# Transposes of two 512 by 128 inputs moved from the matrix engine to memory and VectorE, in a graph network with a mixture of experts

## The chip, the cores and the metric

The kernel runs on one core of one Trainium2 chip. The metric is the device time of one execution in microseconds (us). A core has four compute engines that run their own instruction streams: TensorE (PE in the profile, with its weight loads as PEld), VectorE (DVE), ScalarE (ACT) and GpSimd (POOL). SyncE (SP) issues the DMAs, which 16 DMA engines carry out. Engines wait for each other by semaphores only.

## The reference

`x` is 16 batches of 512 nodes with 128 features, `adj` is 512 by 512. All is float32.

```python
def _layernorm(x, axis=-1, eps=1e-05):
    m = jnp.mean(x, axis=axis, keepdims=True)
    v = jnp.var(x, axis=axis, keepdims=True)
    return (x - m) / jnp.sqrt(v + eps)

# graph network, input x0 = layernorm(x)
h = jnp.einsum('bnd,ed->bne', x, fc_in_w) + fc_in_b
w_eff = w * d_clamped @ w.T
def euler_step(h, _):                       # 8 steps
    ax = jnp.einsum('nm,bmd->bnd', adj_mx, h)
    f = alph * 0.5 * (ax - h) + h @ w_eff - h + x0
    return (h + dt * f, None)

# experts, tokens z = layernorm(x + graph network)
logits = tokens.astype(jnp.float32) @ router_w.astype(jnp.float32).T
probs = jax.nn.softmax(logits, axis=-1)
rw, re = jax.lax.top_k(probs, TOP_K)        # 2 of 8 experts
...
for e in range(E):
    h = jax.nn.gelu(tokens @ w1[e] + b1[e], approximate=False)
    y = h @ w2[e] + b2[e]
    out = out + combine[:, e:e + 1] * y
...
x = x + gnn(layernorm(x)); x = x + ffn(layernorm(x))
```

## The kernel before, in words

**Groups.** The 16 batches are worked in 8 groups of GB = 2. A short set-up builds the operators: the 8 linear steps are folded into powers of the node operator (`LT`) and of the feature operator (`M`). Each float32 factor is split in a high part and a low part, and each product is three TensorE matmuls (`mm3`, L985 to L987). ScalarE makes the high part (`high`, L376), VectorE subtracts it for the low part (`low`, L550).

**One iteration.** Iteration g runs, on TensorE in this order: `nodes_product(3)` (12 matmuls, L985 to L987 with x0s); eight Q items of 9 matmuls (128x384), which read the transposed normalised input `GT[:, b, 0]` and three node products of it; two passes of `horner` (128x256); and then `experts(g-1)`, the experts of the group before. So the two halves of the network are one group apart: while the experts of group g-1 run, VectorE normalises the tokens z of group g and the kernel prepares group g+1. The iterations 1 to 6 are one loop body ("steady" in what follows; `more` is true in them); 0 and 7 are written out apart, and the experts of group 7 follow.

**Experts.** There are 16 items (2 batches by 8 experts). For item i TensorE makes the up product (3 matmuls on zT, w1s), ScalarE the gelu (L484) and the high part, VectorE the weighting `scale_item` (L854, which multiplies by the expert's weight of each token, broadcast to all partitions by DMA) and the low part `item_low` (L550, scs), and TensorE the down product (3 matmuls on scs, w2s), LAG = 5 items behind the up product. A down product waits for the low part of its item.

**Transposes.** The matmuls need the features on the partitions. `transpose_x0` (L1004) turns x0 of group g+1 and `transpose_z` (L1119) turns z of group g with TensorE, four 128x128 transposes for each batch, into PSUM banks; ScalarE and VectorE read them from there as high and low part. In a steady iteration z is turned after up products 10 and 11 and x0 after item 15. `transpose_out` (L1125) turns the experts' sums back.

**Routing.** `logits` (L1111, 8 matmuls) is issued after the first `transpose_out`. VectorE then runs `route_start` (one transpose of 128x256 and three small operations) and `route_on` in the parts 0 to 3 (5, 4, 4 and 4 small operations), each waiting for the one before: `route_start` after `add_out(h, 0)`, part 0 after the low parts of x0, part 1 between the low parts of the node products, and the parts 2 and 3 behind Q items 0 and 1 of the next iteration. The last one gives `comb_out`, which SP stores to memory (L298) and loads back broadcast to all partitions (L290).

**What sets the order.** The streams are written out by hand; each engine runs its instructions in that order and stands still at a wait. On SP, too, everything behind a wait waits.

Of the kernel before, what the change touches and what calls it, by code (L numbers as in the profile page):

```python
# [44 lines left out]
def build(nc, x, adj, alpha, w, d, fc_w, fc_b, router_w, w1, b1, w2, b2, comb_rows, out):  # L45
# [15 lines left out]
    with ctx:  # L61
# [31 lines left out]
        x0s = sb("x0s", [P, 2, NT, GB, D], F32R)  # L93
        GT = sb("GT", [P, GB, BABY, 2, N], F32R)
# [15 lines left out]
        shift = sb("shift", [P, T])  # L110
        zT = sb("zT", [P, 2, GB, N], F32R)
# [3 lines left out]
        lgT = sb("lgT", [P, T, R])  # L115
        cc = sb("cc", [P, T, 4, E])
        combT = sb("combT", [P, H], F32R)
# [59 lines left out]
        x0t_mm, x0t_hi, x0t_lo = sem("x0t_mm"), sem("x0t_hi"), sem("x0t_lo")  # L177
        gt_mm, gt_hi, gt_lo = sem("gt_mm"), sem("gt_hi"), sem("gt_lo")
# [8 lines left out]
        zt_moved = sem("zt_moved")  # L187
        lg_mm, rt_own, rt_pre, rt_tanh, comb_ready = (sem(n) for n in ("lg_mm", "rt_own", "rt_pre", "rt_tanh", "comb_ready"))
# [29 lines left out]
        Z_SCALE, Z_ITEM = 4, 10  # L218
        UP_BANK, SUM_BANK = [4, 5, 6], [0, 1]
# [32 lines left out]
        def _(sp):  # L252
# [39 lines left out]
            def expert_weights(h, g=None):  # L292

                sp.wait_ge(comb_ready, h + 1)
                for b in range(GB):
                    for half in range(2):
                        last = quarter(b, half) + R
                        sp.dma_start(comb_rows[bass.ds(h, 1), b, :, half * H:(half + 1) * H].rearrange("o e n -> (o e) n"),  # L298
                                     comb_out[last - E:last, :]).then_inc(comb_stored, 16)
                if g is not None:  # L300
                    sp.wait_ge(q_ready, T * g + T)
                else:
                    sp.wait_ge(sc_ready, ITEMS * h)
                sp.wait_ge(comb_stored, 64 * h + 64)
                if g is not None:
                    replicate(h, 0, 2, 0, 0)
                    replicate(h, 1, 4, 0, 2)
# [12 lines left out]
            with sp.Fori(1, GROUPS - 2) as g:  # L320
                expert_weights(g - 1, g)
                next_x(g + 2)
                store(g - 1)
            for g in range(GROUPS - 2, GROUPS):
                expert_weights(g - 1, g)
# [48 lines left out]
        def _(act):  # L374
# [29 lines left out]

            def high_gt(g, k, turn):
# [47 lines left out]
            def high_z(g, b, banks=ZT_BANK):  # L453
                act.wait_ge(zt_mm, GB * g + b + 1)
                high(zt_part(0, b), bank[banks[b]][:, :]).then_inc(zt_hi, 1)

# [20 lines left out]
            def experts(h, g=None, more=False):  # L477

                for i in range(ITEMS):
# [10 lines left out]
                    if i == Z_ITEM + 1 and g is not None:  # L490
                        high_z(g, 0)
                    if i == ITEMS - 4:
                        copy_sum(h, 0)
                    if i == Z_ITEM + 2 and g is not None:
                        high_z(g, 1)
                item_high(h, ITEMS - 1)
                if more:
                    high_x0t(g + 1)
# [766 lines left out]
```

## Time and profile before

| | us |
|---|---|
| median of 3 runs | 552.48 |
| lowest, highest | 551.25, 553.32 |
| the profiled execution, device time | 553.18 |
| its span from first to last instruction | 551.4 |
| TensorE busy | 536.2 (97%) |
| VectorE busy | 440.0 (80%) |
| ScalarE busy | 302.8 (55%) |
| GpSimd busy | 53.2 (10%) |
| DMA: share of 16 engines | 23.7% |
| mean granted TensorE clock | 0.996 |

The time is the profiled execution's own device time; the span is what the trace covers. The chain of work that ended last is 86% TensorE and 7% VectorE. In the timeline views a row gives its start and its duration; the next instruction of the same engine may start before the last one has ended, so the step from start to start is what an instruction takes from its engine, and start plus duration is when its result is there for others. An instruction of TensorE shows its latency; 128x512 matmuls follow each other every 0.23 us.

### The profile page before, as it was taken

The page shows a single profiled execution, that of the slowest core. Times are in us where ns is not written, and L with a number is a line of the kernel's source. Part 1 is how long each engine was busy: PE and PEld are TensorE (multiplying, and loading weights), DVE is VectorE, ACT ScalarE, POOL GpSimd, SP SyncE. Part 2 cuts the span into 40 slices and gives each one's busy share as a digit, 9 for nine tenths or more (in the row PEclk, how much of TensorE's full clock was granted, in tenths as well). Part 3 has the DMA queues.
Part 4 walks back from the last instruction along what each step waited for, and adds up shares of the span by engine and source line. Part 5 has one row for each costly group of instructions (what it writes and reads, how often), then busy time and mean ns, then how long its engine had stood idle before and what let it go on. Part 6 is the DMA issues. An engine that isn't in the chain of part 4 may idle for free.

```text
span 551.4 us, 9181 instructions
## 1 busy us (share of the span) xinstructions
PE 536.2 (97%) x2943; PEld 467.1 (85%) x2943; DVE 440.0 (80%) x1128; ACT 302.8 (55%) x525; POOL 53.2 (10%) x42
## 2 busy tenths in 40 slices
PE   5999999999999999999999999999999999999796
PEld 4788997988899788987899788987899788988585
DVE  6988778689866996689866996689866995489995
ACT  5323433468535783468535783468445782148584
POOL 1102011100110101110110101110110101010100
PEclk9999999999999999999999999999999999999999
DMA  4030010072104501172104501162104401160141
GB/s 128 4 112 1 0 40 0 23 246 79 39 3 152 190 0 38 30 244 71 38 2 152 190 0 38 38 236 71 38 2 152 152 4 35 59 233 17 42 191 39
DMA packets 26078, 43.15 MB, mean 78 GB/s; under 512 B 1622, under 2 KB 20684, under 8 KB 24140
## 3 DMA queue, kind: packets, MB, share of 16 engines
q1 hardware_dynamic: 26060, 42.93, 23.7%
q8 instruction: 9, 0.15, 0.1%
q14 instruction: 9, 0.07, 0.0%
HBM read 38.46 MB, written 4.46 MB: 78 GB/s over the span
## 4 chain that ended last, share of the span: by engine, by line
PE 86%; DVE 7%; issue 4%; ACT 2%; POOL 1%; DMA 1%; SPq 0%; POOLq 0%; DVEq 0%
PE bank L985 27%; PE bank L987 26%; PE bank L986 26%; DVE scs L550 2%; PE bank L1111 1%; DVE work L854 1%; PE bank L1125 1%; PE bank L1004 1%; PE bank L1119 1%; DMA work<-in_adj_dram 1%; DVE scr L579 1%; PE bank L1013 1%; PE bank L1171 1%; ACT x L384 1%; POOL scr L355 0%
## 5 line engine op out<-in xcount | busy, mean ns | idle before, releaser
L376 ACT ACTIVATE scs<-work 128x512 fp32r<-128x512 f32 x132 | 83.3, 632 | 24.8 <-DVE work L854 23.8
L484 ACT ACTIVATE work<-bank,cols 128x512 f32<-128x512 f32 x128 | 87.0, 680 | 17.7 <-PE bank L987 17.6
L550 DVE TENSOR_TENSOR scs<-work,scs 128x512 fp32r<-128x512 f32 x132 | 90.8, 689 | 1.9 <-ACT scs L376 0.5
L985 PE MATMUL bank<-M,GT 128*128 128x384 f32 x192 | 64.3, 335 | 0.8 <-DVE GT L550 0.8
L987 PE MATMUL bank<-M,GT 128*128 128x384 f32 x192 | 64.2, 335 | 0.0
L986 PE MATMUL bank<-M,GT 128*128 128x384 f32 x192 | 64.2, 334 | 0.0
L854 DVE TENSOR_TENSOR work<-work,GT 128x512 f32<-128x512 f32 x90 | 61.2, 686 | 2.9 <-ACT work L484 2.3
L376 ACT ACTIVATE GT<-bank 128x512 fp32r<-128x512 f32 x48 | 27.5, 592 | 60.1 <-PE bank L987 57.5
L346 POOL TENSOR_TENSOR rstd<-ve,nhalf 128x8 f32<-128x8 f32 x16 | 30.5, 1908 | 291.1 <-DVE ve L570 291.1
L550 DVE TENSOR_TENSOR GT<-bank,GT 128x512 fp32r<-128x512 f32 x48 | 32.3, 689 | 29.1 <-ACT GT L376 28.8
L911 DVE TENSOR_TENSOR Q<-bank,bias 128x384 f32<-128x384 f32 x64 | 35.4, 552 | 24.9 <-PE bank L987 23.9
L985 PE MATMUL bank<-zT,w1s 128*128 128x512 f32 x128 | 53.0, 414 | 0.2
L985 PE MATMUL bank<-scs,w2s 128*128 128x512 f32 x128 | 52.7, 412 | 0.2 <-DVE scs L550 0.2
L985 PE MATMUL bank<-LT,x0s 128*128 128x512 f32 x128 | 51.4, 402 | 0.0
L986 PE MATMUL bank<-zT,w1s 128*128 128x512 f32 x128 | 51.1, 399 | 0.0
L987 PE MATMUL bank<-zT,w1s 128*128 128x512 f32 x128 | 50.9, 397 | 0.0
L987 PE MATMUL bank<-scs,w2s 128*128 128x512 f32 x128 | 50.6, 396 | 0.0
L986 PE MATMUL bank<-scs,w2s 128*128 128x512 f32 x128 | 50.4, 393 | 0.0
L987 PE MATMUL bank<-LT,x0s 128*128 128x512 f32 x128 | 50.0, 390 | 0.0
L986 PE MATMUL bank<-LT,x0s 128*128 128x512 f32 x128 | 49.9, 390 | 0.0
L376 ACT ACTIVATE scs<-Q 128x512 fp32r<-128x512 f32 x16 | 10.1, 634 | 59.5 <-DVE Q L911 59.5
L985 PEld LDWEIGHTS bank<-M,GT 128*128 128x128 f32 x192 | 36.0, 188 | 1.5 <-DVE GT L550 1.1
(184 smaller groups left out, 1229.0 us busy)
## 6 DMA issues: line engine op xcount, KB each, us to landing
GT<-comb_rows SPq DMA_DIRECT2D x8, 1536.0 KB, 7.2
Q<-comb_rows SPq DMA_DIRECT2D x16, 512.0 KB, 6.2
GT<-comb_rows SPq DMA_DIRECT2D x7, 1024.0 KB, 6.3
xn<-in_x_dram SPq DMA_DIRECT2D x16, 256.0 KB, 7.8
out_dram<-outs SPq DMA_DIRECT2D x16, 256.0 KB, 2.3
GT<-comb_rows SPq DMA_DIRECT2D x7, 512.0 KB, 4.3
work<-in_adj_dram SPq DMA_DIRECT2D x4, 256.0 KB, 3.5
work<-in_L_ffn_w_dram SPq DMA_DIRECT2D x2, 512.0 KB, 5.8
```

What stands on the lines that cost most here:

```text
L346: nc.gpsimd.tensor_tensor(rstd[:, n, :], ve[:, n, :], nhalf[:, :], ALU.pow).then_inc(ln_rstd[n], 1)
L376: return nc.scalar.activation(dst, src, ACT.Copy)
L384: last = nc.scalar.activation(x0[:, t // GB, t % GB, :], xn[:, t // GB, t % GB, :], ACT.Identity, bias=shift[:, t:t + 1], scale=rstd[:, 0, ...
L484: nc.scalar.activation(hid[:, i % 2, :], bank[UP_BANK[i % 3]][:, :], ACT.Gelu, bias=cols[:, B1_COL + e:B1_COL + e + 1]).then_inc(gelu_done, 1)
L550: return v.tensor_tensor(dst, src, hi.bitcast(FP32), ALU.subtract)
L579: return v.tensor_scalar(dst[:, t // GB, t % GB, :], src[:, t // GB, t % GB, :], mv[:, n, 0, t:t + 1], rstd[:, n, t:t + 1], ALU.add, ALU.mult)
L854: v.tensor_tensor(scaled[:, i % 3, :], hid[:, i % 2, :], bank[REP_BANK[i % 2]][:, :] if by_pe else rep(i), ALU.mult).then_inc(sc_ready, 1)
L911: v.tensor_tensor(Q[:, :, t, b, :], src, bias[:, t], ALU.add).then_inc(q_ready, 1)
L985: pe.matmul(dst, wh, xh, start=start, stop=False)
L986: pe.matmul(dst, wh, xl, start=False, stop=False)
L987: return pe.matmul(dst, wl, xh, start=False, stop=stop)
L1004: last = pe.transpose(bank[banks[b]][:, t * P:(t + 1) * P], x0[:, t, b, :], ident[:, :])
```

## The change

In the steady iterations the x0 of the next group and the z of this one are no longer turned by TensorE. SP writes them to memory (`keep_x0`, `blocks_of_z`), as rows of 128 features, and reads them back in pieces of 32 features (128 bytes), so that each 32 by 32 block lies at its transposed place (`blocks_of_x0`: 4 DMAs for both batches into `x0q`; `blocks_of_z`: 4 for each batch into `zq`). VectorE transposes inside the blocks (`turn_x0`, `turn_z`, 128x512 each) into `x0t` and `zt`, and the high and low parts are made from these. VectorE waits in `turn_x0(g, 0)` for all of x0q; it stands after the addition of `xg` (L941 of before), the second one stands in item 0 of the experts, and `low_x0(g+1, 1)` now stands behind the first.

The routing is moved: `logits` is issued after `nodes_product(1)`, `route_start` at the iteration's end, and the four parts behind Q items 0, 1, 3 and 4 of the next iteration. ScalarE's tanh for it (L459) stands at the head of the iteration, and `copy_comb` behind the second high part of y2. In iterations 0 and 7 the transposes stay on TensorE.

```diff
+            def keep_x0(g):
+                sp.wait_ge(x0_ready, g + 1)
+                for b in range(GB):
+                    sp.dma_start(x0_rows[b].rearrange("(t p) c -> p t c", p=P), x0[:, :, b, :]).then_inc(x0_kept, 16)
+            def blocks_of_x0(g):
+                sp.wait_ge(x0_kept, 32 * (g - 1))
+                sp.wait_ge(x0t_lo, GB * g)
+                blocks = x0_rows.rearrange("b (i q) (j a) -> j q (b i) a", q=32, a=32)
+                for j in range(4):
+                    sp.dma_start(x0q[32 * j:32 * (j + 1), :, :].rearrange("p b (i a) -> p (b i) a", a=32),
+                                 blocks[j]).then_inc(x0q_in, 16)
...
                 if g is not None:
                     replicate(h, 0, 2, 0, 0)
+                    if more:
+                        blocks_of_x0(g + 1)
                     replicate(h, 1, 4, 0, 2)
...
+            def turn_x0(g, b):
+                if b == 0:
+                    dve.wait_ge(x0q_in, 64 * (g - 1))
+                    dve.wait_ge(x0t_lo, GB * g)
+                v.transpose(x0t[:, b, :], x0q[:, b, :]).then_inc(x0_turned, 1)
...
+            def turn_z(g, b):
+                dve.wait_ge(zq_in[b], 64 * g)
+                v.transpose(zt[:, b, :], zq[:, b, :]).then_inc(z_turned, 1)
...
+                    if i == 0 and more:
+                        turn_x0(g + 1, 1)
-                    if i in (Z_ITEM + 1, Z_ITEM + 2) and g is not None:
+                    if i in (Z_ITEM + 1, Z_ITEM + 2) and g is not None and not more:
                         low_z(g, i - Z_ITEM - 1)
...
-                    if s == ITEMS and more:
-                        pe.wait_ge(x0_ready, g + 2)
-                        transpose_x0(0)
-                    if s == ITEMS + 1 and more:
-                        pe.wait_ge(gelu_done, ITEMS * h + ITEMS - 2)
-                        transpose_x0(1)
...
-                    if s in (Z_ITEM, Z_ITEM + 1) and g is not None:
+                    if s in (Z_ITEM, Z_ITEM + 1) and g is not None and not more:
                         transpose_z(g, s - Z_ITEM)
                     if s == ITEMS - 1:
                         transpose_out(h, 0)
-                        if g is not None:
+                        if g is not None and not more:
                             logits(g)
...
                 transpose_out(h, 1)
                 if more:
                     nodes_product(1)
-                    pe.wait_ge(x0t_lo, GB * g + 2 * GB)
+                    logits(g)
                     nodes_product(2)
```

VectorE, end of the experts in the steady iteration, before. The scs rows are low parts of items, zT_next is the second low part of z, outs the result of batch 0, lgT the logits, GT<-bank0 and GT<-bank5 are the low parts of x0, rt is routing.

```order
TENSOR_TENSOR scs<-work,scs 128x512
TENSOR_TENSOR zT_next<-bank3,zT_next 128x512
...
TENSOR_TENSOR scs<-work,scs 128x512 x2
...
TENSOR_TENSOR outs<-bank2,scr 128x512
STREAM_TRANSPOSE lgT<-bank7 128x256
...
TENSOR_TENSOR GT<-bank0,GT 128x512
TENSOR_TENSOR GT<-bank5,GT 128x512
SCALAR_TENSOR_TENSOR rt<-rt,rank 128x64
```

Low parts of z stand in the item loop, and routing begins behind the result. The same place in the changed kernel, with zt and x0t the turned blocks:

```order
TENSOR_TENSOR scs<-work,scs 128x512 x2
...
TENSOR_TENSOR outs<-bank2,scr 128x512
STREAM_TRANSPOSE zt<-zq 128x512 x2
TENSOR_TENSOR GT<-x0t,GT 128x512 x2
TENSOR_TENSOR zT<-zt,zT 128x512
TENSOR_TENSOR zT_next<-zt,zT_next 128x512
```

The two low parts of z have left the item loop and stand behind the first addition of the result; the routing has left this place.

VectorE, Q items 2 to 4 of the steady iteration, changed kernel (Q the items' outputs, ve the variance of the next x, rm, cc and comb_out routing). Before, no routing stood between these items.

```order
TENSOR_TENSOR Q<-bank0,bias 128x3x128
...
SCALAR_TENSOR_TENSOR ve<-mv 128x8
...
TENSOR_TENSOR Q<-bank1,bias 128x3x128
TENSOR_SCALAR rm<-rm 128x8
...
TENSOR_TENSOR Q<-bank2,bias 128x3x128
TENSOR_TENSOR cc<-rt 128x8x8
...
STREAM_TRANSPOSE comb_out<-cc 128x256
```

Parts 2 and 3 of the routing came from behind items 0 and 1, where parts 0 and 1 stand now.

SP, steady iteration, changed kernel, from the store of the experts' weights on (x_rows is x0_rows).

```order
DMA x_rows<-x 128x4x128 x2
...
DMA GT<-comb_rows 128x1024
...
DMA x0q<-x_rows 32x32x32 x4
...
DMA GT<-comb_rows 128x2048
```

The four loads of x0q stand between the first and the second load of the experts' weights; the z loads (8 of 32x16x32) come after the load of the next x.

## Rows read from the trace of the kernel before

**Rows 1.** The page: busy time of the engines, and VectorE in 40 slices.
```profile
PE 536.2 (97%) x2943; PEld 467.1 (85%) x2943; DVE 440.0 (80%) x1128; ACT 302.8 (55%) x525; POOL 53.2 (10%) x42
DVE  6988778689866996689866996689866995489995
```

**Rows 2.** The chain that ended last: start us, us, what (L1004 transpose_x0, L1111 logits).
```profile
140.49 0.44 PE bank L1004 x4
...
201.22 1.16 PE bank L1111 x8
202.39 0.44 PE bank L1004 x4
```

**Rows 3.** Timeline of VectorE, experts: start us, us, instruction [idle before <-releaser].
```profile
181.64 1.31 DVE L854 TENSOR_TENSOR work<-work,GT 128x512 f32<-128x512 f32 x2 [0.30 <-ACT work L484]
...
190.99 0.68 DVE L550 TENSOR_TENSOR scs<-work,scs 128x512 fp32r<-128x512 f32 x1
...
198.03 0.69 DVE L550 TENSOR_TENSOR scs<-work,scs 128x512 fp32r<-128x512 f32 x1
198.63 0.69 DVE L550 TENSOR_TENSOR zT<-bank,zT 128x512 fp32r<-128x512 f32 x1
...
204.04 1.48 DVE L550 TENSOR_TENSOR scs<-work,scs 128x512 fp32r<-128x512 f32 x2
205.44 0.68 DVE L842 TENSOR_TENSOR outs<-bank,scr 128x512 f32<-128x512 f32 x1
```

**Rows 4.** Timeline of TensorE: down products of items 5 and 15, then nodes_product(0).
```profile
191.72 0.51 PE L985 MATMUL bank<-scs,w2s 128*128 128x512 f32 x1
192.06 0.40 PE L986 MATMUL bank<-scs,w2s 128*128 128x512 f32 x1
...
205.90 0.40 PE L985 MATMUL bank<-scs,w2s 128*128 128x512 f32 x1
...
206.60 0.40 PE L985 MATMUL bank<-LT,x0s 128*128 128x512 f32 x1
```

**Rows 5.** Timeline of VectorE: routing part 0, then the Q items.
```profile
146.66 0.22 DVE L805 SCALAR_TENSOR_TENSOR rt<-rt,rank 128x64 f32<-128x64 f32 x1
...
147.68 0.22 DVE L811 TENSOR_REDUCE rm<-rt 128x8 f32<-128x64 f32 x1
...
157.04 0.69 DVE L550 TENSOR_TENSOR GT<-bank,GT 128x512 fp32r<-128x512 f32 x1 [0.61 <-ACT GT L376]
...
162.34 0.17 DVE L570 SCALAR_TENSOR_TENSOR ve<-mv 128x8 f32<-128x8 f32 x1
...
168.44 0.69 DVE L550 TENSOR_TENSOR x0s<-x,x0s 128x512 fp32r<-128x512 f32 x1 [0.67 <-ACT x0s L376]
...
170.30 0.69 DVE L550 TENSOR_TENSOR scs<-Q,scs 128x512 fp32r<-128x512 f32 x1 [0.70 <-ACT scs L376]
```

**Rows 6.** Timeline of ScalarE: x0 of the next group.
```profile
164.55 3.20 ACT L384 ACTIVATE x<-xn,shift,rstd 128x128 f32<-128x128 f32 x8 [0.48 <-POOL shift L349]
```

**Rows 7.** Timeline of TensorE: first matmul that needs the second low part of y2.
```profile
171.38 0.28 PE L985 MATMUL bank<-scs,LT 128*128 128x256 f32 x1
```

**Rows 8.** Timeline of VectorE: the addition of xg and the first x1.
```profile
175.63 1.22 DVE L941 TENSOR_TENSOR Q<-Q,xg 128x1024 f32<-128x1024 f32 x1
178.04 0.42 DVE L950 TENSOR_TENSOR Q<-bank,Q 128x256 f32<-128x256 f32 x1 [1.19 <-PE bank L987]
```

**Rows 9.** Groups by line and shape: busy us, mean ns of one | idle before.
```profile
L832 DVE STREAM_TRANSPOSE comb_out<-cc 128x256 f32<-128x256 f32 x8 | 3.6, 446 | 1.3 <-DVE cc L828 1.2
```

**Rows 10.** DMA from 144 to 147 us: packets, MB, share of 16 engines; an issue.
```profile
q1 hardware_dynamic: 528, 0.26, 29.1%
...
out_dram<-outs SPq DMA_DIRECT2D x1, 256.0 KB, 2.3
```

**Rows 11.** DMA from 161 to 165 us, the four stores of 8 KB.
```profile
q1 hardware_dynamic: 64, 0.03, 3.8%
```

**Rows 12.** Timeline of SP: first and second load of the experts' weights.
```profile
169.77 0.95 SPq L290 DMA_DIRECT2D GT<-comb_rows  x2
```

More of the change, by code:

```diff
@@ L93, in build @@
         x0s = sb("x0s", [P, 2, NT, GB, D], F32R)
+        x0q = sb("x0q", [P, GB, N])
+        x0t = sb("x0t", [P, GB, N])
         GT = sb("GT", [P, GB, BABY, 2, N], F32R)
@@ L187, in build @@
         zt_moved = sem("zt_moved")
+        z_kept, zq_in, z_turned = sem("z_kept"), [sem(f"zq_in{b}") for b in range(GB)], sem("z_turned")
         lg_mm, rt_own, rt_pre, rt_tanh, comb_ready = (sem(n) for n in ("lg_mm", "rt_own", "rt_pre", "rt_tanh", "comb_ready"))
@@ L403, in high_x0t, with high_turned @@
                     high(GT[:, b, 0, 0, :], bank[banks[b]][:, :]).then_inc(x0t_hi, 1)
+            def high_turned(g):
+                for b in range(GB):
+                    act.wait_ge(x0_turned, GB * (g - 2) + b + 1)
+                    high(GT[:, b, 0, 0, :], x0t[:, b, :]).then_inc(x0t_hi, 1)
             def high_gt(g, k, turn):
@@ L509, in iteration @@
                     high(y2s[:, 0, 2 * p:2 * p + 2], Q[:, 2, 2 * p:2 * p + 2]).then_inc(y2_hi, 1)
-                    if p == 0 and not first:
+                    if p == 1 and not first:
                         copy_comb(g - 1)
@@ L530, in iteration @@
                     if not final:
-                        high_gt(g + 1, 0, 0)
-                        route_tanh(g)
-                        for k in range(1, 3):
+                        for k in range(3):
                             high_gt(g + 1, k, k)
@@ L880, in experts @@
                     for b in range(GB):
-                        low_x0t(g + 1, b)
-                    route_on(g, 0)
+                        turn_z(g, b)
+                    for b in range(GB):
+                        low_turned(g + 1, b)
+                    for b in range(GB):
+                        low_turned_z(g, b)
                     low_gt(g + 1, 0, 0)
@@ L889, in experts @@
                     low_gt(g + 1, 1, 1)
-                    route_on(g, 1)
                     low_gt(g + 1, 2, 2)
+                    route_start(g)
             def iteration(g, first=False, final=False):
                 if not first and not final:
-                    for b in range(GB):
-                        norm_x_stats(g + 1, b)
+                    norm_x_stats(g + 1, 0)
                 if not first:
                     low_gt(g, 3, 3)
+                if not first and not final:
+                    norm_x_stats(g + 1, 1)
                 def low_y2(p):
@@ L922, in iteration @@
                 low_y2(1)
-                if not final:
+                if first:
                     low_x0(g + 1, 1)
@@ L941, in iteration @@
                 v.tensor_tensor(Q[:, 0], Q[:, 0], xg[:, :, :, :], ALU.add).then_inc(xq_ready, 1)
+                if not first and not final:
+                    turn_x0(g + 1, 0)
+                    low_x0(g + 1, 1)
                 def x1_stats(t):
@@ L1176, in experts @@
                         transpose_out(h, 0)
-                        if g is not None:
+                        if g is not None and not more:
                             logits(g)
```

70 lines of the change are left out of this document (51 added, 19 removed).

## The prediction

> **What bounds the kernel now.** I read the page first: TensorE is busy 97% of the span, VectorE 80%, and VectorE's slices swing between 6 and 9 or more [rows 1]. A share like that hides stretches in which VectorE is full. The chain that ended last gives the period of the steady loop: the transposes of x0 start at 140.49 and at 202.39, so one iteration takes 61.90 us, and there are six of them [rows 2]. I then went through one iteration on the timelines, stretch by stretch, and asked of each TensorE instruction how early its operand had been there.
>
> In the experts VectorE has no idle time. From item 0 at 181.64 to the end of the low part of item 15 at 204.04 + 1.48 = 205.52 its 128x512 operations follow every 0.60 us (198.03, 198.63), though none waits for TensorE; the one wait is 0.30 us ahead of the first [rows 3]. The stretch is 23.88 us long. TensorE is as full, but only just: the down product of item 15 starts at 205.90, 0.38 us after its low part, and the one of item 5 at 191.72, 0.05 us after its low part ended at 190.99 + 0.68 [rows 3, 4]. So in the experts both engines are full at once, and after them TensorE alone: behind 206.60 it has 11 us of node products, in which VectorE often waits.
>
> **What TensorE gives up.** Four transposes take 0.44 us of the chain [rows 2]. A steady iteration drops four such sets, 1.76 us; six iterations 10.6 us. That is the ceiling. All four sets stood in the experts, and the 1.16 us of the logits [rows 2] leave them too, so TensorE's work between item 0 and the last down product shrinks by 2.92 us.
>
> **What VectorE gets in that stretch.** It loses the two low parts of z (2 x 0.60) and gains one turn of x0. No row shows a transpose of 128x512; the one of 128x256 takes 446 ns [rows 9]. Doubled it is 0.89 us; if it grows with the columns as the other operations do, it is 0.69 with a step of 0.62. I take 0.62, since the step between VectorE's neighbours of that size is 0.60 [rows 3]. The stretch becomes 23.88 - 1.20 + 0.62 = 23.30 us. The low part of item 15 ends 0.58 us earlier, at 204.94 on the old scale, while TensorE would be there at 205.90 - 2.92 = 202.98. It stands for 2 us.
>
> A matmul that stood shows its price at item 5: it starts 0.05 us after its operand and the next follows after 0.34 instead of 0.23 us, 0.11 more [rows 4]. The down product of item 15 then takes 0.70 + 0.11 us (205.90 to 206.60 was 0.70), and the first node product starts at 204.94 + 0.05 + 0.81 = 205.80 instead of 206.60. **Gain 0.80 us** out of 2.92. The addition of the result, which this product also waits for, starts 0.08 us ahead of the low part's end [rows 3] and is done 0.60 us behind it, in time.
>
> **What comes back.** The logits now stand between the node products, where TensorE is the limit: **+1.16 us**. Their operands: from 204.86 VectorE runs the addition, two turns of z (0.62), two low parts of x0 and two of z (0.60 each), done near 209.2; the logits come at 205.80 + 2.75 + 0.44 + 2.75 = 211.7. The moved work at this end is covered by 2.5 us, and so is a z block that is late by as much.
>
> **The Q items.** Here VectorE gets the parts 0 and 1 more. Part 0 takes 1.24 us (146.66 to 147.68 + 0.22) [rows 5], part 1 with its four operations 1.0. I walk it on the old scale: route_start fills the gap in front of the low part at 157.04, which is 0.61 us long there with the statistics ahead of it [rows 5]; half of the statistics (0.8 us) now follow it. 157.64 + 0.82 (four statistics), Q item 0 0.47, part 0 1.24, Q item 1 0.47, part 1 1.03, Q item 2 0.45 gives 162.1; the variance ends at 163.0 instead of 162.34 + 0.17 = 162.51, **0.48 us later**. TensorE's items need only the one four places back, ready by over a microsecond. But GpSimd, ScalarE's x0 (164.55 before [rows 6]), the low part of x0 that VectorE waits for at 168.44, Q item 7 behind it and the second low part of y2 at 170.30 hang on the variance one behind the other, each with a wait in front of it [rows 5]. The last ends at 170.99 + 0.48 = 171.47; TensorE wants it at 171.38 [rows 7]. **+0.1 to 0.2 us, with the 0.11 of a stalled matmul: 0.2.** The parts 2 and 3 lie behind item 3 and end before 166.0; the weights' stores are then 5 us later than now, but their loads wait for Q item 7 in either case.
>
> **Turning x0 ahead of the x1 additions.** VectorE idles 1.19 us before 178.04 [rows 8]. The turn (0.62) and low_x0 (0.60) take 1.22. Hidden, if x0q is there at 175.63 + 1.12 = 176.75. With the shift of 0.2 and the 0.3 us idle ahead of item 0 [rows 3], a landing up to 177.2 costs nothing; each microsecond after that is a microsecond of VectorE and, since the experts are bound by it, of the iteration. When does it land? ScalarE's x0 is done at 164.55 + 3.20 + 0.48 = 168.23. SP stores it in two DMAs of 256 KB; an issue takes 0.48 [rows 12] and a store of this kind lands 2.3 us after its issue [rows 10]: 171.1 to 171.4. Four loads are issued from then on, behind the first 512 KB of the weights in the same queue (issued near 170.2, in flight to about 172.9). 4096 packets over 16 engines are 256 for each: the landing is about 173.1 + 0.256 c us for c ns a packet, and 177.2 is met up to **c = 16 ns**. No row has packets of 128 bytes. Those of 512 bytes took 0.291 x 3 us x 16 / 512 = 27.3 ns [rows 10]; in proportion to bytes that is 6.8 ns, the lower bound. 27.3 is what a quarter of the bytes cannot well exceed if packets stream; the 64 packets of the small stores, half of them a few bytes, took 0.038 x 4 x 16 / 64 = 38 ns [rows 11], the outer bound. Waits: 0, 2.9 and 5.6 us an iteration. I take it as hidden, since the 512-byte packets run near what larger ones do in bytes, so most of their 27 ns is bytes; but only narrowly.
>
> The page "DMA: Bandwidth & Descriptors" of the Trainium skill, section "Why small descriptors are slow (HBM only)", gives a packet three cycles beside one for every 32 bytes: 7 against 19, an estimate of 10 ns here, hidden. Its section "Specifications" asks for 512 bytes for line rate; if shorter packets cost as much as one of 512, c is 27.3. The page "VectorE: DVE Perf Modes", section "Rules for kernel authors", speaks against the change: turn 128x128 on TensorE where PSUM will do.
>
> **The sum.** -0.80 + 1.16 + 0.20 = +0.56 us an iteration, six times 3.4 us. The iterations 0 and 7 and the last experts keep their transposes, and the moved routing parts in 7 find VectorE with nothing to prepare: nothing. 553.18 + 3.4 = 556.6 for an execution like the profiled one, which lies 0.70 above the median; on the median **555.9 us**. Bounds without the wait for x0q: +0.8 (no stall at y2, no 0.11, logits at 1.05) and +7 (turns at 0.89 and each handover 0.1 dearer): 553.3 to 559.5.
>
> **Rivals.** *x0q lands late.* For it: the margin is 0.4 us, and four DMAs with short pieces behind 512 KB of weights; against it: the proportion to bytes. The wait decides from c = 16 ns. At 27.3 ns, 6 x 2.9 = 17.4 us: 573.3; at 38 ns 6 x 5.6: 589.5. The late queue also pushes the second load of the weights, which item 2 needs at 184.5; it has some 3 us.
> *Faster.* VectorE's rhythm of 0.60 us might be TensorE's, handed on through the gelus. Then both shorten and all of 1.76 us comes in: 552.5 - 10.6 = 541.9. Against it: VectorE's pairs keep 0.60 where nothing is waited for [rows 3].
> *z lands late.* Stored after 193.9, its 4096 packets need to land by 206 plus 2.5 us of cover; that takes c over 40 ns. 560 or more.
>
> **Chances.** Hidden, 555.9: 0.49. Late x0q, 560 to 590: 0.38, of it 0.09 above 574. Faster: 0.08. Late z or else: 0.05. The range 551.5 to 574 leaves out some 2 in 10. A difference of 0.5%, 2.8 us, is about what a measurement of this kernel can tell; the hidden case lies at +3.4, so 0.2 of its 0.49 fall within it. Faster by more 0.09, within 0.24, slower 0.67.
>
> **What would show it.** In the profile after: TensorE waits for the low part (L603, scs) ahead of down products, 1 to 2 us an iteration, with the period between two sets of logits at 62.4 to 62.5; VectorE at a step of 0.60 through all 16 items; a wait of 0.1 us ahead of the second part of y2. Idle time ahead of the first STREAM_TRANSPOSE x0t, released by a DMA, decides the rival, and the packets' mean gives c. A period under 61.9 with VectorE full would prove the reading of the experts wrong.

## The result and the profile after

The changed kernel takes 554.97 us (median of 9 runs, 554.67 to 557.52) against 553.02 us for the kernel before in the same 9 comparisons. The ratio is 1.0058, with a 95% interval of 1.0044 to 1.0072: slower, by 3.2 us by the ratio; the two medians lie 1.95 us apart. The forecast was 555.9 us in a range of 551.5 to 574.0, and slower.

The page of the changed kernel, busy time and slices of VectorE, answers to [rows 1]:

```profile
span 552.9 us, 9116 instructions
...
PE 532.6 (96%) x2847; PEld 452.9 (82%) x2847; DVE 449.4 (81%) x1152; ACT 304.6 (55%) x525; POOL 53.2 (10%) x42
...
DVE  6988687789686995799776995799776995689995
```

TensorE ran its 96 transposes less, VectorE is 9.4 us busier, and the span is 1.5 us longer than the 551.4 before. Where the time went is read from the period. I take the first matmul of the eight Q items in each iteration from TensorE's timeline (us from the span's start; from iteration 1 to iteration 7, the last one, lie the six steady periods):

| kernel | it. 1 | it. 2 | it. 3 | it. 4 | it. 5 | it. 6 | it. 7 | six periods |
|---|---|---|---|---|---|---|---|---|
| before | 92.52 | 156.07 | 217.99 | 279.89 | 341.79 | 403.69 | 465.63 | 373.11 |
| changed | 91.22 | 154.03 | 217.09 | 279.86 | 342.31 | 404.76 | 467.31 | 376.09 |

The six periods are 2.98 us longer, close to the 3.2 us of the ratio. What lies around them differs from one execution to the next: iteration 1 begins at 91.33 to 92.93 us in the traces of the kernel before and of its variants, at 90.94 to 93.05 in those of the changed kernel and its variants. So small differences between kernels are read from the periods below, beside the ratio. The first period is 0.74 us shorter (62.81 for 63.55), the others are 1.14, 0.87, 0.55, 0.55 and 0.61 us longer. For the period from 217.09 to 279.86 (62.77 us) I cut as the prediction did.

**The experts.** VectorE's timeline, first item and end of the experts, answers to [rows 3]:

```profile
243.50 0.68 DVE L925 TENSOR_TENSOR work<-work,GT 128x512 f32<-128x512 f32 x1
244.09 0.70 DVE L675 STREAM_TRANSPOSE x0t<-x0q 128x512 f32<-128x512 f32 x1
244.72 0.65 DVE L925 TENSOR_TENSOR work<-work,GT 128x512 f32<-128x512 f32 x1
245.29 0.68 DVE L603 TENSOR_TENSOR scs<-work,scs 128x512 fp32r<-128x512 f32 x1
...
264.53 0.68 DVE L925 TENSOR_TENSOR work<-work,Q 128x512 f32<-128x512 f32 x1
265.13 1.47 DVE L603 TENSOR_TENSOR scs<-work,scs 128x512 fp32r<-128x512 f32 x2
266.52 0.68 DVE L913 TENSOR_TENSOR outs<-bank,scr 128x512 f32<-128x512 f32 x1
```

From 243.50 to 265.13 + 1.47 = 266.60 are 23.10 us (23.88 before). In between VectorE never idles for more than 0.1 us; the longest pause, 0.09 us, is ahead of the low part of item 15, and it was there before.

The stretch is 0.2 us shorter than the 23.30 us of the prediction. That is read at its start: in the kernel before the first low part starts here, released by ScalarE's high part:

```profile
183.03 0.69 DVE L550 TENSOR_TENSOR scs<-work,scs 128x512 fp32r<-128x512 f32 x1
```

This is 1.39 us after item 0 at 181.64, behind two operations with a step of 0.60 us, so about 0.2 us of it is waiting. In the changed kernel it comes 1.79 us after item 0, with the turn (a step of 0.62) ahead of it and no wait. The turn costs the stretch 0.40 us.

TensorE's timeline at the same place, the end of the experts, answering to [rows 4]:

```profile
264.22 0.40 PE L1066 MATMUL bank<-scs,w2s 128*128 128x512 f32 x1
264.67 0.50 PE L1064 MATMUL bank<-scs,w2s 128*128 128x512 f32 x1
...
265.87 0.50 PE L1064 MATMUL bank<-scs,w2s 128*128 128x512 f32 x1 [0.23 <-DVE scs L603]
...
266.68 0.47 PE L1064 MATMUL bank<-scs,w2s 128*128 128x512 f32 x1
266.99 0.39 PE L1065 MATMUL bank<-scs,w2s 128*128 128x512 f32 x1
...
267.46 0.39 PE L1064 MATMUL bank<-LT,x0s 128*128 128x512 f32 x1
```

The down products of items 13 and 14 start 0.45 and 0.63 us behind the matmul ahead of them instead of 0.23: TensorE waits for one low part after the other. That of item 15 starts 0.08 us after its operand, the node products 0.86 us after it (1.08 before).

**The logits.** They stand between the node products, now 0.96 us long ([rows 2] had 1.16):

```profile
210.63 0.65 PE L1190 MATMUL bank<-zT,rts 128*128 128x256 f32 x4
211.11 0.64 PE L1190 MATMUL bank<-zT_next,rts 128*128 128x256 f32 x4
211.59 0.40 PE L1064 MATMUL bank<-LT,x0s 128*128 128x512 f32 x1
```

From the first node product to the first Q item it is 12.39 us (204.70 to 217.09), 11.37 before: +1.02.

**Q items and x0q.** VectorE's timeline, answering to [rows 5] and [rows 8]; the waits for ScalarE's x0 and for y2 are there, and one for a DMA:

```profile
223.99 0.17 DVE L623 SCALAR_TENSOR_TENSOR ve<-mv 128x8 f32<-128x8 f32 x1
...
230.09 0.69 DVE L603 TENSOR_TENSOR x0s<-x,x0s 128x512 fp32r<-128x512 f32 x1 [1.30 <-ACT x0s L417]
...
231.95 0.69 DVE L603 TENSOR_TENSOR scs<-Q,scs 128x512 fp32r<-128x512 f32 x1 [0.70 <-ACT scs L417]
...
237.08 1.22 DVE L1018 TENSOR_TENSOR Q<-Q,xg 128x1024 f32<-128x1024 f32 x1
239.42 0.71 DVE L675 STREAM_TRANSPOSE x0t<-x0q 128x512 f32<-128x512 f32 x1 [1.12 <-DMA x0q<-x_rows]
```

From the first Q item to item 0 of the experts it is 26.41 us instead of 25.57. TensorE starts the second part of the first horner pass at 232.69, 15.60 us after the Q items' start; [rows 7] has it 15.31 after. And x0q is late in each of the six iterations: VectorE waits 1.61, 1.23, 1.12, 0.81, 0.86 and 0.93 us for it. The stretches sum up: -0.78 (experts) - 0.22 (from there to the node products) + 1.02 (logits) + 0.84 (Q items to item 0) = +0.86, the period's 62.77 less 61.90 within the rounding. All that the change costs lies in them.

### The profile page after: what moved, and what is told of

Same layout as the page of the kernel before. It is cut to its first block, busy times and chain, and to the rows that moved or that the text cites. A ratio compares the mean times of both kernels' runs of the same rounds, so it can differ in the third digit from the quotient of the medians.

```text
span 552.9 us, 9116 instructions
## 1 busy us (share of the span) xinstructions
PE 532.6 (96%) x2847; PEld 452.9 (82%) x2847; DVE 449.4 (81%) x1152; ACT 304.6 (55%) x525; POOL 53.2 (10%) x42
## 4 chain that ended last, share of the span: by engine, by line
issue 32%; PE 29%; DVE 25%; ACT 4%; POOL 4%; DMA 3%; SPq 2%; DVEq 0%; POOLq 0%
PE bank L1064 9%; PE bank L1066 9%; PE bank L1065 9%; DVE scs L603 8%; DVE work L925 5%; ACT x L425 3%; POOL scr L396 2%; DVE bn L607 2%; DVE scr L632 2%; POOL rstd L387 2%; DVE Q L1031 2%; DMA x0q<-x_rows 2%; DMA x_rows<-x 1%; SPq L311 1%; ACT scs L417 1%
## 5 line engine op out<-in xcount | busy, mean ns | idle before, releaser
L1064 PE MATMUL bank<-scs,w2s 128*128 128x512 f32 x128 | 55.8, 436 | 3.1 <-DVE scs L603 1.7
L417 ACT ACTIVATE GT<-bank 128x512 fp32r<-128x512 f32 x36 | 21.1, 595 | 61.7 <-PE bank L1066 59.2
L603 DVE TENSOR_TENSOR GT<-bank,GT 128x512 fp32r<-128x512 f32 x36 | 24.4, 686 | 35.2 <-ACT GT L417 35.1
L1066 PE MATMUL bank<-scs,w2s 128*128 128x512 f32 x128 | 50.7, 396 | 0.0
L1065 PE MATMUL bank<-scs,w2s 128*128 128x512 f32 x128 | 50.3, 393 | 0.0
L1064 PEld LDWEIGHTS bank<-scs,w2s 128*128 128x128 f32 x128 | 24.0, 187 | 25.1 <-DVE scs L603 21.4
L1064 PE MATMUL bank<-scs,LT 128*128 128x256 f32 x128 | 36.3, 283 | 0.8 <-DVE scs L603 0.3
```

The costliest lines, as they stand in the source:

```text
L417: return nc.scalar.activation(dst, src, ACT.Copy)
L603: return v.tensor_tensor(dst, src, hi.bitcast(FP32), ALU.subtract)
L1064: pe.matmul(dst, wh, xh, start=start, stop=False)
L1065: pe.matmul(dst, wh, xl, start=False, stop=False)
L1066: return pe.matmul(dst, wl, xh, start=False, stop=stop)
```

## The experiments

The kernels run beside the kernel before; every ratio is to that. Periods are the six as in the table.

**1. Fewer transposes, nothing else.** The kernel before with one transpose of four left in each set of a steady iteration.

```diff
-                        transpose_x0(0)
+                        transpose_x0(0, tiles=1)
...
-                        transpose_z(g, s - Z_ITEM)
+                        transpose_z(g, s - Z_ITEM, tiles=1 if more else NT)
```

> The kernel before, with one of the four 128x128 transposes left in each of the four sets of a steady iteration; the other three of each set are left out, so those columns of x0 and z stay what the bank held. TensorE loses 12 transposes of 0.11 us, 1.3 us an iteration and 7.9 us in all; nothing is moved. Theory (VectorE bounds the experts): only the 0.38 us ahead of the last down product can be had, at most 2.3 us in all, ratio 0.996 to 1.000, and TensorE idles ahead of the down products instead. Rival (VectorE's rhythm is TensorE's, handed on): 7.9 us, ratio 0.986, and VectorE's stretch from item 0 to the last low part falls from 23.9 to under 23 us.

Ratio 0.9978 (0.9962 to 0.9994), 1.2 us; the steady periods are 61.67 to 61.71 us, 0.2 less. TensorE's weight loads waited for the low parts 36 times instead of 12. The waits of the kernel before, and then of this one:

```profile
PEld bank L985 <- DVE scs L550: 4.7, 12, 0.7
```

```profile
PEld bank L985 <- DVE scs L550: 14.4, 36, 1.1
```

The first number is the sum over the trace, the second how often, the third the longest. Of 7.9 us that TensorE no longer works, 1.2 are gained; VectorE's stretch is 23.88 us long as before. The rival by which VectorE's rhythm was TensorE's handed on has fallen: TensorE's transposes were nearly free where they stood, as soon as it is a question of taking them away.

**2. The logits twice.**

```diff
-                    logits(g)
+                    logits(g, 2)
```

> The changed kernel with the eight logits matmuls issued twice in the steady iterations (the second set writes the same result again). In the trace of the changed kernel they take 0.96 us, from 210.63 to 211.59. Theory (the place between the node products is bound by TensorE, so what is moved there is paid in full): +0.96 us an iteration, +5.8 us in all, ratio to the kernel before near 1.016. Rival (VectorE bounds the whole iteration, TensorE has room everywhere): no more than +1 us, ratio near 1.007.

Ratio 1.0176 (1.0156 to 1.0196), 6.5 us over the changed kernel. The second set starts 0.95 us after the first (213.20 after 212.25), and the six periods are 5.82 us longer than the changed kernel's, 0.97 each. The place is paid for in full.

**3. The turns of x0 behind the experts.**

```diff
-                    turn_x0(g + 1, 0)
                     low_x0(g + 1, 1)
...
-                    if i == 0 and more:
-                        turn_x0(g + 1, 1)
...
                 add_out(h, 1)
                 if more:
+                    for b in range(GB):
+                        turn_x0(g + 1, b)
                     low_gt(g + 1, 1, 1)
+                    for b in range(GB):
+                        low_turned(g + 1, b)
```

ScalarE's high parts of x0 move with them.

> The changed kernel with both turns of x0 on VectorE, their high and low parts, moved behind the experts, between the low parts of the node products, where the trace of the changed kernel shows VectorE idle for 1.9 and 3.1 us. Nothing waits for x0q any more at the x1 additions (1.1 us of waiting an iteration in that trace), and one turn of 0.6 us leaves the stretch that VectorE bounds. Theory (both sit on the path): -0.55 to -0.9 us for the wait and -0.6 for the turn, 7 to 9 us in all off 555, 546 to 548, ratio 0.988 to 0.992: faster than the kernel before. Rival (the late x0q is hidden in the slack before the experts): only the turn, 3.6 us, ratio 0.999. Rival (TensorE is the bound in the experts): nothing, 1.006.

Ratio 0.9964 (0.9943 to 0.9984): 5.2 us better than the changed kernel and 2.0 us better than the kernel before. The six periods are 371.73 us, the steady ones 62.00. The direction is the theory's; the size, 0.9 us an iteration, is less than the 1.15 to 1.5 expected, and by the periods it is 4.36 / 6 = 0.73. Both shares were overpriced. The turn's departure shortens VectorE's stretch from 23.10 to 22.74 us, 0.36 instead of 0.6, because the wait of 0.2 us that it had filled is back: the first low part comes 1.39 us after item 0 again. The share of the wait for x0q is read from run 6.

**4. The variance first.**

```diff
-                    if not first and not final and i == 2:
+                    if not first and not final and i == 0:
                         ln_var(0, g + 1)
```

> The changed kernel with the variance of the next x taken behind Q item 0, ahead of the routing parts, instead of behind item 2. GpSimd's root, ScalarE's x0, its stores and x0q come 3.3 us earlier than in the changed kernel. Theory (variance to x0 to Q item 7 to the second low part of y2, and x0q, are one chain that the moved routing made late): the gap of TensorE ahead of the second part of the first horner pass (0.3 us) and the wait for x0q (1.1 us, of which some 0.6 is paid) both go: -0.8 to -1.0 us an iteration, 5 to 6 us off 555, ratio 0.995 to 0.998. Rival (that chain costs nothing, the loss is the logits alone): 0, ratio 1.006.

Ratio 0.9998 (0.9984 to 1.0012), 3.3 us better than the changed kernel, with 5 to 6 expected. TensorE's pause ahead of the second part of the horner pass is gone. But the wait for x0q only went from 6.6 to 4.9 us over six iterations. The expectation had the chain come 3.3 us earlier; the variance does come 3.0 earlier, ScalarE's x0 only 1.0: it stands behind the high part of y2 (the output of the Q items that the first horner pass reads) in ScalarE's stream, which waits for Q item 3. And x0q lands only 0.84 us earlier; the next run shows what it lands by.

VectorE's timeline of this kernel (Q items from 217.81), then ScalarE's:

```profile
221.71 0.17 DVE L623 SCALAR_TENSOR_TENSOR ve<-mv 128x8 f32<-128x8 f32 x1
```

```profile
225.38 0.63 ACT L417 ACTIVATE scs<-Q 128x512 fp32r<-128x512 f32 x1 [2.10 <-DVE Q L988]
225.92 3.18 ACT L425 ACTIVATE x<-xn,shift,rstd 128x128 f32<-128x128 f32 x8
```

**5. x0's stores ahead of the weights' stores on SP**, added to run 4.

```diff
+                if more:
+                    keep_x0(g + 1)
                 sp.wait_ge(comb_ready, h + 1)
...
-                if more:
-                    keep_x0(g + 1)
                 if g is not None:
```

> The run with the variance behind Q item 0 (ratio 0.9998), and x0's stores issued ahead of the stores of the experts' weights on SP, instead of behind them. In that run SP issued the weights' stores from 228.05 to 229.76 and x0's at 229.87, though x0 was ready some 2 us earlier, and VectorE still waited 0.7 to 1.5 us for x0q. Theory (x0q is late because its stores stand in SP's queue behind the moved routing): x0q lands 1.5 to 2 us earlier, the wait goes, -0.4 to -0.7 us an iteration, ratio 0.993 to 0.996. Rival (the four loads' own time, behind q_ready and the first load of the weights, sets the landing): nothing changes, 1.000.

Ratio 1.0185 (1.0145 to 1.0225), 1.9% worse than run 4: both theory and rival fell. SP's timeline of this kernel, whose Q items start at 220.80:

```profile
232.11 0.92 SPq L303 DMA_DIRECT2D x_rows<-x  x2
233.24 1.88 SPq L334 DMA_DIRECT2D comb_rows<-comb_out  x4
236.15 0.38 SPq L297 DMA_DIRECT2D GT<-comb_rows  x1
236.75 4.07 SPq L311 DMA_DIRECT2D x0q<-x_rows  x4
```

x0 is ready 11.3 us after the Q items' start, only 0.75 us ahead of where SP stored it in run 4. The weights, ready at 230.87, now wait behind it, so their first load is issued 15.35 us after the start instead of 13.43 and x0q's loads with it; VectorE waits 2.6 us an iteration for x0q (15.4 us in six). A wait for a late event had been put in front of an early one.

The traces of these runs show more than the argument about x0's stores. In us behind the issue of the first load of the weights (iteration 3):

| kernel | first x0q issue | third x0q issue, start | and end | weights landed | x0q landed |
|---|---|---|---|---|---|
| changed | 1.33 | 2.31 | 4.12 | 4.38 | 7.98 |
| run 4 | 2.08 | 3.07 | 3.91 | 4.06 | 8.03 |
| run 5 | 0.60 | 1.57 | 4.05 | 4.38 | 8.09 |
| run 6 (half of x0q) | 1.34 | 2.25 | 2.74 | 4.26 | 6.32 |

Whether x0q's loads are issued 0.60 or 2.08 us behind the weights' load makes no difference to when they land. They stand behind it in the queue, and by these traces its landing and their own packets set theirs. So the rival was right in what sets the landing, and wrong in that nothing would change, since the edit delayed the load ahead too.

**6. Half of x0q.**

```diff
-                blocks = x0_rows.rearrange("b (i q) (j a) -> j q (b i) a", q=32, a=32)
+                blocks = x0_rows[0].rearrange("(i q) (j a) -> j q i a", q=32, a=32)
...
-                    sp.dma_start(x0q[32 * j:32 * (j + 1), :, :].rearrange("p b (i a) -> p (b i) a", a=32),
+                    sp.dma_start(x0q[32 * j:32 * (j + 1), 0, :].rearrange("p (i a) -> p i a", a=32),
```

> The changed kernel with the second batch's half of x0q left out (the four loads move 64 KB each, 2048 pieces of 128 bytes instead of 4096; the other half stays zero, so half of the transposed x0 is wrong). Theory (the pieces' number sets both the issue on SP, 0.85 us each of four, and the landing): an issue takes 0.5 us, x0q lands over 1.5 us earlier, VectorE's wait of 1.1 us goes, -0.5 to -0.7 us an iteration, 3 to 4 us off the changed kernel, ratio 0.999 to 1.001. Rival (the landing is set by the stores, their receipt and the queue of the weights): the wait stays over 0.7 us, ratio 1.004 to 1.006.

Ratio 1.0033 (1.0015 to 1.0052), 1.4 us better than the changed kernel by the ratios, whose intervals overlap; 3 to 4 were expected. The four issues take 1.93 us instead of 3.40, x0q lands 1.66 us earlier behind the weights' load, and VectorE does not wait for it at all. SP's timeline of the changed kernel, and then of this one:

```profile
232.75 3.40 SPq L311 DMA_DIRECT2D x0q<-x_rows  x4
```

```profile
232.93 1.93 SPq L311 DMA_DIRECT2D x0q<-x_rows  x4
```

The theory's mechanism holds in part: fewer pieces shorten the issues and the landing, but both stay behind the weights' load. The gain is smaller than its price: without the wait the six periods are 373.90 us, 2.2 less than the changed kernel's, though the waits were 6.6 us long. The last four are 62.36 to 62.38, as good as the 62.45 with waits of 0.8 to 0.9 us. Some 0.7 us of each wait, (6.6 - 2.2) / 6, was hidden after all. In run 6 VectorE pauses 0.23 us ahead of the second x1 addition and 0.30 ahead of item 0; from start to start these two steps are 0.32 and 0.38 us longer than in the changed kernel, where the late x0q fills them. Only what is over that is paid. Runs 4 and 5 agree: from the first Q item to item 0 of the experts it is 25.57 us in run 4 with waits of 0.7 us, as in the kernel before without any, and 27.54 in run 5 with one of 2.69, 1.97 more.

**7 and 8. VectorE relieved by one microsecond**, in the changed kernel and in the kernel before.

```diff
-                for t in (2 * half, 2 * half + 1):
+                for t in (2 * half, 2 * half + 1) if every else (2 * half,):
...
-                        scale_z(g, (i - Z_SCALE) // 2, (i - Z_SCALE) % 2)
+                        scale_z(g, (i - Z_SCALE) // 2, (i - Z_SCALE) % 2, False)
```

> The changed kernel with half of the normalisation of z left out in iterations 1 to 7 (4 of its 8 operations of 128x128, so half of the tokens keep old values). VectorE loses 4 steps of 0.25 us, 1.0 us, in the experts; nothing else changes. Theory (VectorE bounds the experts of the changed kernel, TensorE stands for 1 to 2 us there): nearly all comes back, -0.9 us an iteration, 5 to 6 us off the changed kernel, ratio to before 0.995 to 0.997. Rival (TensorE is the bound, its pauses are made up later): 0, ratio 1.006.

> The same half of z left out of the kernel before. Theory (both engines are full there, TensorE with 0.38 us of room at the last down product): next to nothing, 0 to -0.1 us an iteration, ratio 0.998 to 1.000. Rival (VectorE alone bounds the experts before as well): -0.9 us an iteration, ratio 0.989.

The changed kernel falls to a ratio of 0.9921 (0.9892 to 0.9950), 7.6 us below the changed kernel, for 7 iterations with 1.0 us of VectorE each: us for us. In the six periods it is 6.58 us, and VectorE's stretch is 22.10 us long instead of 23.10. The kernel before falls to 0.9937 (0.9917 to 0.9958); its steady periods are 61.46 to 61.50 us, 0.4 less. That is neither the next to nothing of the theory nor the 0.9 of the rival. VectorE's stretch is 1.02 us shorter, but the first node product comes 1.66 us behind it instead of 1.08, so TensorE bounds it now. What it gains are two pauses of TensorE in the kernel before: 0.2 us at the down product of item 5, where its step ahead and its step after are 0.32 and 0.34 us instead of 0.23, and 0.2 us ahead of the logits, which wait for the second low part of z. The prediction had seen the first; the second is this line of the kernel before, which run 8 does not have:

```profile
PEld bank L1111 <- DVE zT_next L550: 1.4, 7, 0.2
```

Runs 1 and 8 together say that in the kernel before either engine alone can be relieved for 0.2 to 0.4 us only.

**9 and 10. All of z's normalisation on GpSimd**, in the changed kernel with the edits of runs 3 and 4, and in the kernel before.

```diff
-                        scale_z(g, (i - Z_SCALE) // 2, (i - Z_SCALE) % 2)
...
+                for b in range(GB):
+                    for t in range(NT):
+                        k = GB * t + b
+                        last = nc.gpsimd.tensor_scalar(z[:, t, b, :], x1[:, t, b, :], mv[:, 1, 0, k:k + 1],
+                                                       rstd[:, 1, k:k + 1], ALU.add, ALU.mult)
+                    last.then_inc(z_ready, 1)
```

> The changed kernel with all that the theory says it lacks: the two turns of x0 behind the experts and the variance of x behind Q item 0, as in the two runs of before, and the eight operations that normalise z on GpSimd, which is idle then, instead of VectorE. VectorE loses 2.0 us more in the experts, so TensorE should be the bound in the whole iteration, with 1.76 us less to do than in the kernel before. Theory: a period of 60.2 to 60.6 us instead of 61.9, 8 to 10 us off the kernel before, ratio 0.982 to 0.986. Rival (GpSimd and VectorE get in each other's way, or z comes so late that its blocks miss their place): VectorE's steps grow over 0.60 us while GpSimd works, ratio 0.99 or more.

> The kernel before with the normalisation of z on GpSimd alone. VectorE gets 2.0 us of room in the experts. Theory (TensorE is the bound there as soon as VectorE isn't): no more than its small pauses, 0 to 0.2 us an iteration, ratio 0.997 to 1.000. Rival (VectorE is the one bound): -1.9 us an iteration, ratio 0.976.

Ratios 1.0291 (1.0259 to 1.0323) and 1.0435 (1.0397 to 1.0472): both theories failed. GpSimd's timeline in run 9, and VectorE's there:

```profile
252.60 15.22 POOL L406 TENSOR_SCALAR scr<-Q,mv,rstd 128x128 f32<-128x128 f32 x8
```

```profile
273.75 0.71 DVE L917 STREAM_TRANSPOSE zt<-zq 128x512 f32<-128x512 f32 x1 [4.68 <-DMA zq<-z_rows]
```

In run 10 the first wait is TensorE's, for z:

```profile
PE bank L1131 <- POOL scr L365: 20.6, 10, 2.3
```

One operation takes 1.9 us in run 9, z is ready at 267.8 and its blocks are missing at the end of the experts. VectorE's steps went from 0.60 to 0.70 us for only one in three. The rival's second half, z too late, is what happened; the GpSimd operation's price had been taken from nothing. The price is not one number either. In run 10 the durations in ns, lowest, median and highest, are

```profile
L365 POOL TENSOR_SCALAR scr<-Q,mv,rstd x56: 442/1700/1922, 125.5 to 529.0; 128x128 f32<-128x128 f32 x56
```

1.91 us is what one takes while VectorE runs its 128x512 operations of the items back to back, three in that time. From 199.75 us VectorE is idle for 2.02 us, and there GpSimd's operations take 0.44 us each. So GpSimd works here at a quarter of its pace as long as VectorE runs these operations.

In run 9 the wait costs more than its length. TensorE stands 2.76 us ahead of the logits, and its granted clock is then at the lower of its two levels, 1.2 GHz, for 3.4 us: the eight logits matmuls take 1.78 us instead of 0.96, and the matmuls behind them follow every 0.43 us instead of 0.23.

```profile
278.19 1.13 PE L1201 MATMUL bank<-zT,rts 128*128 128x256 f32 x4 [2.76 <-DVE zT_next L617]
...
279.97 0.63 PE L1075 MATMUL bank<-LT,x0s 128*128 128x512 f32 x1
280.40 0.63 PE L1076 MATMUL bank<-LT,x0s 128*128 128x512 f32 x1
```

**11. Both edits**, of runs 3 and 4.

> The changed kernel with both earlier edits: the turns of x0 behind the experts, and the variance of x behind Q item 0. The first alone gave a steady period of 62.0 us (62.5 in the changed kernel, 61.9 before), with TensorE's gap ahead of the second part of the first horner pass still there; the second alone removed that gap. Theory (they are separate costs): 61.7 us, 1.8 us off the first alone, ratio to before 0.992 to 0.994. Rival (VectorE's walk to the experts is what counts, the gap is made up there): 62.0, ratio 0.996.

Ratio 0.9935 (0.9910 to 0.9960), 548.58 us. The steady periods are 61.52 to 61.59 us. The theory holds: the two are separate costs. VectorE's stretch is 22.74 us as in run 3, and from the first Q item to item 0 of the experts it is 25.57 us as in run 4.

**12. Two of z's eight operations on GpSimd**, on top of run 11, in the steady iterations.

```diff
-                for t in (2 * half, 2 * half + 1):
+                for t in (2 * half, 2 * half + 1) if not shared or b == 0 else (half,):
...
+                    for t in (2, 3):
+                        k = GB * t + 1
+                        last = nc.gpsimd.tensor_scalar(z[:, t, 1, :], x1[:, t, 1, :], mv[:, 1, 0, k:k + 1],
+                                                       rstd[:, 1, k:k + 1], ALU.add, ALU.mult)
+                    last.then_inc(z_shared, 1)
```

> As the run with both edits, and in the steady iterations two of the eight operations that normalise z (the last two of batch 1) on GpSimd, where one took 1.85 us; VectorE's loop loses 0.5 us. z is ready no later, since GpSimd needs 3.7 us behind the root and VectorE's own come 4 to 6 us behind it. Theory (VectorE's time in the experts is the bound, us for us): -0.5 us an iteration less about 0.2 for VectorE steps of 0.70 instead of 0.60 beside GpSimd, 1.8 us off the run with both edits, ratio 0.989 to 0.991. Rival (GpSimd disturbs VectorE as much as it relieves it): no gain, 0.993.

Ratio 0.9894 (0.9870 to 0.9919), 546.22 us: faster than both kernels, by 1.1% and 1.6%. GpSimd's two take 1.89 us together here. 0.5 us less for VectorE in six iterations gave 2.3 us over run 11; the two intervals touch, but the six periods, 367.18 for 369.38 us, agree.

## Why the prediction was right

**What bounds the experts: right.** Of TensorE's 2.92 us the prediction expected 0.80 back, 0.58 from VectorE's shorter stretch and 0.22 behind it. It was 0.78 + 0.22 = 1.00. Run 1 shows it without the rest of the change, run 7 from the other side. The 0.2 us too little is a wait that the prediction had not seen when it wrote that the only one is ahead of the first item: VectorE's 0.2 us ahead of the first low part, which the turn fills. It had also missed TensorE's 0.2 us ahead of the logits (run 8).

**The logits: right, 1.02 us for 1.16.** Run 2 gives 0.95 for one more set in the trace and 6.5 / 6 = 1.1 in the time.

**The chain behind the variance: right.** Foreseen 0.48 us later and a pause of 0.2 us; in the trace the first pass waits 0.29 us longer, with 0.11 more for the stalled matmul, and run 4 removes it. That is 0.4 us where the sum had 0.2. What was not foreseen is a pause of 0.57 us at VectorE's loop end, ahead of the first statistics, which has no counterpart before; the variance lands 6.90 us after the Q items' start plus its 0.17, 7.07, against 6.44 before, 0.63 later instead of 0.48.

**x0q: the rival happened, at a fraction of its price.** The likeliest case had it hidden. The packets cost what a hidden case needs: the z blocks, alone in the queue from 259 to 264 us, took 0.661 x 5 us x 16 / 4224 = 12.5 ns each, under the threshold of 16.

```profile
DMA packets 4224, 0.52 MB, mean 105 GB/s; under 512 B 4224, under 2 KB 4224, under 8 KB 4224
...
q1 hardware_dynamic: 4224, 0.52, 66.1%
```

The page "DMA: Bandwidth & Descriptors" of the Trainium skill, section "Why small descriptors are slow (HBM only)", had led to an estimate of 10 ns; the trace is 12.5 and decides. The step that failed is the load ahead in the queue. The prediction had the first 512 KB of the weights issued near 170.2 and in flight to about 172.9, 2.7 us, and took x0q's packets from 173.1 on. In the changed kernel that load takes 4.4 us (4.3 in the median on the page of either kernel, so the kernel before had it too):

```profile
231.41 0.36 SPq L297 DMA_DIRECT2D GT<-comb_rows  x1
```

```profile
GT<-comb_rows SPq DMA_DIRECT2D x1, 512.0 KB, 4.4
```

It lands at 235.79, which is 174.8 on the scale of the kernel before, and x0q 3.6 us behind it, at 239.4 instead of by 238.2. With 12.5 ns a packet the prediction's formula gives 176.3 on the old scale; it was 178.4.

The four issues of x0q took 3.40 us where the prediction had 1.92, but this is not what made x0q late. The third is held on SP for 1.81 us in the changed kernel, 0.84 in run 4 and 2.48 in run 5, and it is let go at nearly the same time behind the issue of the weights' load: 3.7 to 4.2 us in all 54 sets of issues of the nine kernels that load x0q whole, shortly before that load lands. With half the pieces (run 6) no issue is held. A fixed price for the making of 1024 descriptors would not give 0.84 us in one kernel and 2.48 in another, so the traces speak for the full queue. No run takes the weights' load away; that would be the test.

The prediction then priced a late landing one for one beyond 0.4 us of room; runs 4, 5 and 6 put the room at some 0.7 us.

**The sum: right by two errors, so by luck.** Forecast +0.56 an iteration with x0q hidden, 3.4 us in all; measured 2.98 us over six periods, of which run 6 gives x0q 2.2. Without it the change costs 0.8 us by run 6's periods (1.8 by its ratio): five iterations at 0.44 to 0.54, against a first one that is quicker by 1.6 us. The steady iteration without x0q was forecast well, but part by part (iteration 3, run 6 less the kernel before): -0.76 and -0.22 in the experts for -0.80 together, +1.03 for the logits for 1.16, +0.39 up to item 0 for 0.20.

The first iteration had been taken for a steady one, though its period before was 63.55 us and not 61.90. The traces show why it gets shorter. In the kernel before the routing parts 0 and 1 of the short iteration 0 stand ahead of the statistics of the next x, so the variance comes 8.31 us after the Q items' start instead of 6.44, and the second part of the first horner pass starts after 16.85 us instead of 15.31. In the changed kernel these parts stand behind Q items 0 and 1 and the pass starts after 15.31: 1.54 us less, only in this iteration. This is read from the order of the two traces; no run tests it.

**The faster rival** fell with run 1, the late z with the trace: no wait for zq shows in the changed kernel.

## What to carry to other kernels

Before work is taken from the busiest engine, look in the stretch where that work stands for the second engine that is full as well, and compare when each operand was ready with when it was used: that gap, here 0.38 us, of which run 1 gained 0.2, is all that can be gained there. Work moved out of such a stretch into one that the busiest engine bounds alone is a loss even if nothing is added. What made this change pay in the end was to relieve VectorE in the experts and to put its new work where it was idle; and a DMA should be priced from the landing of what stands ahead of it in the queue, with that load's own time from the page, and then by its packets. A first iteration that differs from the others belongs in the sum by itself.

## What the runs showed of the hardware

Four DMAs with 1024 pieces of 128 bytes each, behind a load of 512 KB in the same queue, held SP for 2.3 to 4.7 us in different kernels, against 1.9 us with 512 pieces each; eight DMAs with 512 pieces each, with nothing ahead of them, held it for 4.04 us, 0.5 us each. A piece of 128 bytes took 12.5 ns of a DMA engine's time, one of 512 bytes 27.3 ns.

GpSimd's 128x128 float32 operation with two scalars for each partition took 0.44 us while VectorE was idle and 1.91 us each while VectorE ran 128x512 operations with two inputs back to back; two of them beside a mix that held such operations and VectorE's own normalisation took 1.40 and 0.50 us. VectorE's step went from 0.60 to 0.70 us for one operation in three meanwhile. VectorE needs 0.25 us for the same operation.

A VectorE transpose of 128x512 took 0.70 us, with a step of 0.62; from the 128x256 one of 0.45 us the prediction had 0.69 and 0.62. After 2.76 us without a matmul TensorE's granted clock was at 1.2 GHz for 3.4 us, with 128x512 matmuls every 0.43 us instead of 0.23 (run 9).
